# Attention and a gated feed-forward block on one core: K stacked SBUF to SBUF in eight transfers a batch, new orders of work, and the last pair's GELU output split by two engines

## The reference

```python
x = x + tanh(g_xattn) * xattn(layernorm(x), ctx)      # softmax(q k^T / 4) v, then wo, biases
x = x + tanh(g_ffn) * ffn(layernorm(x))
# ffn: gelu(x w1 + b1) w2 + b2, times the sum of the two best router weights (renormalised)
```

## Time and profile before

| | us |
|---|---|
| median of three runs | 735.21 |
| the profiled execution, its own time | 734.14 |
| its span | 732.1 |
| TensorE busy in the span | 696.4 (95%) |
| VectorE busy | 514.4 (70%) |
| ScalarE busy | 402.5 (55%) |
| GpSimd busy | 321.3 (44%) |

### The profile page before, as it was taken

One profiled execution on the slowest core, in us unless ns is written; L12 is line 12 of the kernel. 1 busy time (PEld: TensorE's weight loads), 2 busy tenths in 40 slices (PEclk: granted clock), 3 DMA queues, 4 the chain that ended last, 5 costly groups with the idle time before them and its releaser, 6 DMA issues.

```text
span 732.1 us, 20618 instructions
## 1 busy us (share of the span) xinstructions
PE 696.4 (95%) x7648; PEld 652.3 (89%) x7648; DVE 514.4 (70%) x1298; ACT 402.5 (55%) x800; POOL 321.3 (44%) x476
## 2 busy tenths in 40 slices
PE   3688999999999999999999999999999999999987
PEld 2566888999999999999999999999999999988966
DVE  6378788777776777776777777777677777766422
ACT  2124666465564646556564746556474655656753
POOL 4313436444434545434344544343454543424246
PEclk9979999999999999999999999999999999999999
DMA  4868789866748585764658486684758576450000
GB/s 146 179 198 169 187 189 224 155 170 137 178 104 174 125 187 132 171 167 124 158 111 206 103 187 154 129 190 110 165 122 182 139 171 150 104 93 3 15 1 27
DMA packets 84021, 103.21 MB, mean 141 GB/s; under 512 B 9589, under 2 KB 79570, under 8 KB 83922
## 3 DMA queue, kind: packets, MB, share of 16 engines
q1 hardware_dynamic: 83282, 101.12, 59.9%
q10 hardware_dynamic: 640, 0.77, 0.5%
HBM read 65.05 MB, written 34.05 MB: 135 GB/s over the span
## 4 chain that ended last, share of the span: by engine, by line
PE 87%; DVE 4%; ACT 2%; issue 2%; POOL 2%; SPq 1%; DMA 1%; ACTq 0%; POOLq 0%; DVEq 0%
PE P L921 42%; PE S L951 13%; PE T L963 11%; PE OT L978 11%; PE P L1004 4%; PE TR L987 2%; PE TR L1060 1%; DVE NEGM L764 1%; PE TR L1043 1%; ACT PROBS L678 1%; PE TR L994 1%; PE TR L936 1%; DVE XN L832 1%; PE TR L1028 1%; DMA QS<-q_parts 1%
## 5 line engine op out<-in xcount | busy, mean ns | idle before, releaser
L764 DVE TENSOR_REDUCE NEGM<-S 112x1 f32<-112x375 f32 x512 | 267.3, 539 | 73.4 <-PE S L951 71.3
L678 ACT ACTIVATE PROBS<-T 125x448 f32<-125x448 f32 x384 | 196.2, 543 | 106.0 <-PE T L963 98.4
L951 PE MATMUL S<-KS,QS 96*112 96x376 f32 x512 | 181.7, 361 | 9.6 <-DVE NEGM L764 6.3
L963 PE MATMUL T<-QS,KS 98*125 98x224 f32 x768 | 150.6, 282 | 3.1 <-ACT PROBS L678 1.7
L963 PEld LDWEIGHTS T<-QS,KS 98*125 98x125 f32 x768 | 129.3, 188 | 10.0 <-ACT PROBS L678 4.6
L582 POOL CAST HT_HI<-HG 128x224 fp32r<-128x224 f32 x128 | 47.3, 369 | 152.0 <-ACT HG L701 144.0
L951 PEld LDWEIGHTS S<-KS,QS 96*112 96x112 f32 x512 | 91.3, 180 | 23.5 <-DVE NEGM L764 13.0
L566 POOL CAST CT_HI<-CTRAW 128x750 fp32r<-128x750 f32 x31 | 25.1, 810 | 161.7 <-DMA CTRAW<-in_ctxT 151.0
L584 POOL TENSOR_TENSOR HT_LO<-HG,HT_HI 128x224 fp32r<-128x224 f32 x128 | 85.2, 666 | 10.3
L978 PE MATMUL OT<-PROBS,VA 125*17 125x112 f32 x3072 | 87.6, 260 | 0.0
L701 ACT ACTIVATE HG<-P,B 128x224 f32<-128x224 f32 x128 | 57.2, 447 | 53.4 <-PE P L921 52.2
(11 more groups left out here) (113 smaller groups left out, 1496.8 us busy)
## 6 DMA issues: line engine op xcount, KB each, us to landing
KS<-k_parts SPq DMA_DIRECT2D x90, 375.0 KB, 7.1
CTRAW<-in_ctxT SPq DMA_DIRECT2D x32, 375.0 KB, 3.5
k_parts<-KHI SPq DMA_DIRECT2D x30, 375.0 KB, 3.9
k_parts<-KLO SPq DMA_DIRECT2D x30, 375.0 KB, 4.5
QS<-q_parts SPq DMA_DIRECT2D x96, 112.0 KB, 4.9
X<-in_x SPq DMA_DIRECT2D x16, 224.0 KB, 3.6
q_parts<-QHI SPq DMA_DIRECT2D x32, 112.0 KB, 2.4
q_parts<-QLO SPq DMA_DIRECT2D x32, 112.0 KB, 2.3
```

What stands on the lines that cost most here:

```text
L678: act.activation(PT[0:KN, k, pp * 4 * SQ:(pp + 1) * 4 * SQ], T_BANK[i % 2][0:KN, 0:4 * SQ], ACT.Exp, scale=SCALE).then_inc(exp_done, 1)
L764: dve.tensor_reduce(NEGM[:, b.par, i:i + 1], S_BANK[i % 2][0:SQ, 0:SK], AX.X, ALU.max, negate=True).then_inc(max_done, 1)
L951: pe.matmul(S_BANK[i % 2][0:SQ, 0:SKP], QS[0:96, i, b.ring * SQ:(b.ring + 1) * SQ], KS[0:96, b.ring, i // 2, :], start=True, stop=True).th ...
L963: mm = pe.matmul(T_BANK[i % 2][0:KN, r * 2 * SQ:(r + 1) * 2 * SQ], KS[0:98, prv.ring, pair, k * KN:(k + 1) * KN], QS[0:98, 2 * pair:2 * pa ...
```

## The change

**K.** KHI and KLO get 376 columns as KS has. Every batch's K is moved directly from SBUF to SBUF, by four transfers for the high part, each of 32 source partitions written twice to 64 destination partitions, and four for the low part. The stages `ks` and `kl` and the DRAM scratch are gone, `kd` issues the moves on SP (`ka` on ScalarE for batch 0). For that, the rows are laid out anew: low in rows 0 to 31, each high row twice in rows 32 to 95, QS to fit, and the heads' order in V, NEGM and WO follows (`head`).

**Q.** QS is laid out by pair of batches and by half; its loads are as many as before (six a pair) with rows of 448 numbers in place of 224.

**Start.** The first loads are stages (`ld`) in the table, in another order. The clearing is cut into pieces that are stages too (`zp`, `zq`, `zr`, `zi`, `zh`, `zy`, `zv`, `zo`), and each user waits for its piece. w1 and w2 come in eight parts of 512 columns through HG (`lw`, `w`), whose low parts are made by GpSimd, as is that of wv.

**Orders.** Both tables are new throughout.

**The last pair.** For batches 30 and 31 GpSimd splits the even eighths of the GELU output and VectorE the odd ones.

```diff
 def move_k(engine, b, high):
+    for p in (0, 2, 1, 3):
+        slots = KS[32 if high else 0:96 if high else 32, b.ring, DC * p:DC * (p + 1), :]
+        part = (KHI if high else KLO)[32 * p:32 * p + 32, :, :].rearrange("p c n -> p (c n)").bitcast(F32)
+        if high:
+            part = part.unsqueeze(1).to_broadcast([32, 2, DC * SKP])
+        engine.dma_start(slots.rearrange("p c n -> p (c n)").bitcast(F32),
+                         part).then_inc(khi_moved if high else klo_moved, 16)
...
-                    if op == "ks" and nn.exists:
...
-                    if op == "kl" and nn.exists:
...
+                    if op == "kd" and nn.exists:
+                        held(sp, sp_passed, (st_ready, nn.count(12, -36)),
+                             (khi_done if i == 0 else klo_done, nn.count(2, 2)))
+                        move_k(sp, nn, i == 0)
...
+                    if op == "lw":
+                        src, raw_in, _, _ = w_part(i)
                         if i:
-                            sp.wait_ge(w2_split, 2 * i)
+                            sp.wait_ge(w_split, 2 * i)
+                        load(raw_in, src, w_loaded)
...
+                    if op == "w":
+                        _, raw_in, high, low = w_part(i)
+                        pool.wait_ge(w_split, 2 * i + 1)
+                        pool.tensor_tensor(low, raw_in, high.bitcast(F32), ALU.subtract).then_inc(w_split, 1)
...
-                    if op == "lo" and pg.exists:
+                    if op == "lo" and pg.exists and not (pg.k == LAST_PAIR and i % 2):
...
+                    if op == "lo" and pg.k == LAST_PAIR and i % 2:
+                        n = i // 2 + 1
+                        if i == 1:
+                            dve.wait_ge(dn_ready, pg.group(GB))
+                        dve.wait_ge(gelu_done, pg.group(FC, i + 1))
+                        dve.tensor_copy(HT[0][:, i, :], HG[:, i % HR, :]).then_inc(odd_high, 1)
+                        dve.wait_ge(odd_high, n)
+                        dve.tensor_tensor(HT[1][:, i, :], HG[:, i % HR, :], HT[0][:, i, :].bitcast(F32),
+                                          ALU.subtract).then_inc(odd_split, 1)
...
-    (34, """x2t dn.1+2 up.0 up.1 up.2 up.3 up.4 up.5 up.6 lo.0 lo.1 rt rx rw.0 up.7 rw.1 rw.2 dh.0 rw.3 lo.2 rw.4
-       lo.3 lo.4 rw.5 lo.5 dh.1 lo.6 lo.7 rw.6 rw.7 dn.0 dn.1"""),
+    (34, """x2t dn.0+2 lo.6+2 rt dn.1+2 lo.7+2 rx rw.0 up.0 up.1 lo.0 rw.1 lo.1 lo.2 up.2 up.3 lo.3 rw.2 rw.3
+       rw.4 up.4 up.5 lo.4 lo.5 up.6 lo.6 ol-1 rw.5 rw.6 up.7 lo.7 dh.0 rw.7 dh.1 dn.0 dn.1"""),
```

More of the change, by code:

```diff
@@ L46 @@
 LAG = 4
+LAST_PAIR = NB - GB
 RING = 4
@@ L395, in move_k @@
-        def move_k(engine, b, row):
-            part, moved = (KLO, klo_moved) if row == 1 else (KHI, khi_moved)
-            for p in range(4):
-                engine.dma_start(KS[32 * row:32 * row + 32, b.ring, p:NPAIR:4, 0:SK].bitcast(F32),
-                                 part[32 * p:32 * p + 32, :, :].bitcast(F32)).then_inc(moved[b.k], 16)
+        THIRD = NH * SQ
+        WK_IN, WV_IN, WQ_IN = raw(0, DC, D), raw(THIRD, DC, D), raw(2 * THIRD, DC, D)
+        W_IN = HG[:, :, :].rearrange("p r n -> p (r n)")[:, 0:W_PART]
@@ new lines, in w_part, with head @@
+        def w_part(i):
+            if i < 4:
+                c, n = i % 2, slice(W_PART * (i // 2), W_PART * (i // 2 + 1))
+                return w1[c * 128:(c + 1) * 128, n], W_IN, W1[0][:, c, n], W1[1][:, c, n]
+            c = slice(2 * (i - 4), 2 * (i - 3))
+            return (w2[c.start * 128:c.stop * 128].rearrange("(c p) n -> p c n", p=128),
+                    W_IN.rearrange("p (c n) -> p c n", c=2), W2[0][:, c, :], W2[1][:, c, :])
+        def head(h):
+            return 2 * NPAIR // DC * (h // 2 % DC) + 2 * (h // 2 // DC) + h % 2
@@ new lines, in move_k @@
+        def move_k(engine, b, high):
+            for p in (0, 2, 1, 3):
[5 more added lines that the diff above has]
+                                 part).then_inc(khi_moved if high else klo_moved, 16)
@@ L672, in step @@
                         if prv.k == 0 and i == 0:
-                            for split in (wk_split, wq_split, wv_split, w1_split):
+                            for split in (wk_split, wq_split, wv_split):
                                 act.wait_ge(split, 2)
@@ L730, in step @@
                     bank = P_BANK[BANKS.get((now.k, stage), 0)]
-                    if op in SPLIT:
+                    if op == "zp":
+                        for part in CT:
+                            dve.memset(part[:, :, :, SK:SKP].bitcast(F32), 0.0).then_inc(pads_zeroed, 1)
+                    if op == "zq":
+                        dve.memset(QS[:, 0, 1, :, :].bitcast(F32), 0.0).then_inc(qs_high_zeroed, 1)
+                    if op == "zo":
+                        dve.memset(OT[:, :], 0.0).then_inc(ot_zeroed, 1)
+                    if op in SPLIT and op in LOW_ON_DVE:
                         raw_in, parts, _, split = SPLIT[op]
```

355 lines of the change are left out of this document (176 added, 179 removed).

## The result

The changed kernel takes 712.92 us (median of four runs, 711.34 to 717.17), against 734.88 of the kernel before beside it: a ratio of 0.970, with a 95% interval of 0.965 to 0.975. The forecast was 716. Its profiled execution took 713.49 us, with a span of 711.6. Six runs more on another chip gave 712.36 (ratio 0.970, 0.967 to 0.973).

A forecast was written before the change was run, and what follows sets the result against it. TensorE was taken to bound the middle, with gains only at the start and end. Terms -4.8 + 0.7 - 8.3 + 0 - 9 + 3 - 0.7 = -19.1 us gave a 713.0 us span, forecast 716, range 705 to 733.

The forecast's parts named there:

- The start: Up to the first score product: -4.8 us, to 29.5 from 34.3, with wk and context loaded first and less clearing.
- six Q loads by 24.9, and 4.53 us later it is 29.5: Last step of the start: Q loads issued by 24.9 us, landing 4.53 us later, set the first score product.
- Batch 0's scores: First score product to batch 0's `mt`: +0.7 us, 13.5 for 12.8, with 65 matmuls in place of 34.
- 16 maxima, five V biases and some 2.5 us more: 13.2 us: VectorE's work during batch 0's scores: maxima by 0.54 us, V biases by 0.42; taken as 13.5 us.
- The ramp: Batch 0's to batch 5's `mt`: -8.3 us, 96 for 104.3, as the splits of w1 and w2 leave VectorE.
- 29 for these two: In the ramp, batches 1 and 2 together take 29 us, at VectorE's pace of some 14 us each.
- The middle: Batch 5's to batch 29's `mt`: K's new way gives 0, bounds -6 to +6; TensorE waits for no K there.
- The last pair's scores: Batch 29's to 31's `mt`: -9 us, 27 at 0.087 a matmul; then to the last `x2t`: +3, 26.5 for 23.5.
- The end: Last pair's `x2t` to the end: -0.7 us, 19.2 for 19.9, with GELU splits shared by GpSimd and VectorE.
- The weight pieces: Rival, 0.09: SP's seven waits for w1 and w2 pieces delay K or Q by 4 us each: 744 us.
- The steady stretch: Rival, 0.08: the middle holds waits too short to see; 40.8 us a pair, 12 us more gained: 704 us.
- Only the two ends: Rival, 0.17: VectorE's 0.54 us a maximum holds close scores, so -8.3 and -6 shrink to -2 each: about 726 us.

The follow-up runs named there:

- GpSimd waits once: Changed kernel, but GpSimd starts the context split of iteration -1 only when VectorE has scaled the third pair's XN: 711.9 us, ratio 0.967.
- RSTD first: Changed kernel, but in iteration -2 GpSimd makes the second pair's variance and RSTD before the context cast, CT_LO and BO: 712.5 us, ratio 0.969.
- changed kernel again: The changed kernel once more, unaltered, in six runs: 712.4 us, ratio 0.970.
- sixteen moves: Changed kernel with each of the eight K moves of a batch cut into two of half the size: 730.3 us, ratio 0.993.
- twelve moves: The kernel before with its orders, layout and start, only K moved directly by twelve moves a batch: 817.3 us, ratio 1.109.
- XN later: Changed kernel, but VectorE scales the third pair's XN in iteration 0 between the maxima of heads 8 and 9, after KLO: 714.9 us, ratio 0.972.
- three moves: Changed kernel with XN later, GpSimd's RSTD before the context split, and ScalarE's tanh of the gates behind both K halves: 711.4 us, ratio 0.969.

## Why the prediction was right, point by point

- **The start, 29.5 for 29.1: right in size, wrong in the last wait.** The step "six Q loads by 24.9, and 4.53 us later it is 29.5" failed. TensorE's chain of waits (start us, us, what) leads through the second pair's XN and not through the Q loads:

```profile
9.87 4.65 DMA CTRAW<-in_ctxT
...
15.57 1.64 POOL CT_LO L591
17.20 0.93 POOL BO L581
...
18.65 0.73 POOL RSTD L543
19.41 0.75 DVE XN L847 x2
...
20.29 0.98 PE TR L1055 x4
21.27 4.48 PE P L943 x18
```

  I had counted GpSimd's list nowhere in this stretch. The chain goes back to the second context, which SP issues at 9.87 us behind all the first loads and which GpSimd splits before it makes RSTD. The Q loads were issued by 25.3 and landed in 2.7 to 3.3 us where I had put 4.53, so the Q path was some 1 us off being last: with XN earlier by 1.3 us the score products wait for it. That the time agreed within 0.4 us is luck. The first matmul came at 6.8 (forecast 7.5).
- **Batch 0's scores, +0.7 for +4.5: wrong.** The step was the sum "16 maxima, five V biases and some 2.5 us more: 13.2 us" of VectorE's work, with each instruction at its price alone. Without the collision it is right: 13.5, 12.9 and 13.5 us in three profiles (GpSimd waits once, RSTD first, changed kernel again). The prediction used the rule of the shared ports at the last pair and did not look for it here, though the earlier trace rows had wv's low part at 1.84 us.
- **The ramp, -8.3 for -12.3: right in sign, short by a third.** VectorE's relief, on which the term stood, brings 3.9 us. The rest is the order: 92.0 for 117.8 with the same code. The step that failed is "29 for these two": batches 1 and 2 took 24.8 us and not VectorE's pace of 14 each, while the other three took 22.3, 19.2 and 25.7 for 22, 18.5 and 26.5. TensorE is busy for 90.7 of the 92.0 us.
- **The middle, 0 for -3.2: right within its bounds.** Nothing waits for K, a pair takes 41.55 for 41.8, and the difference is the order's, since with the old one it is 41.74. The ten profiles with this order, the one with sixteen moves among them, have 498.0 to 499.7 us here, so up to 1.7 of the 3.2 us differ from one execution to another. The slack in SP's queue is at least the 4.8 us that sixteen moves used up, and it belongs to the order: in the old one twelve moves cost 5.8 us a pair.
- **The last pair's scores, -9 for -6.5; then +3 for +1.9.** Both within bounds. The 29.5 us have 28.8 of TensorE busy, so 313 matmuls cost 0.092 each there and not the 0.087 of the steady stretch, which was the wrong mean for that mix. Together they are -4.6 for -6.
- **The end, -0.7 for +0.3.** The two engines do exclude each other; the splits in turn are worth 1.5 us, and the final additions on GpSimd behind WT set the result at 708.0, which I had put on TensorE's last down projections.
- **The rivals.** The weight pieces do hold SP, but 4.4 us in two waits, where it takes seven of 2.7 to decide; in the old order SP waits 24.1 us for them, and their share of the loss was not measured apart. The steady stretch gains 3.2 us and not 12. "Only the two ends" fell with the ramp.

The sum came out 1.4 us from the span by luck, because +3.8 and -4.0 cancelled. K's way, the headline of the change, gains nothing by itself: in the old orders its eight moves leave the middle as it was, while the whole new code is 10 us slower there, since the ramp loses 13.5 us; twelve moves cost 82 us.

## What to carry to other kernels

A transfer that moves fewer bytes can still cost more queue: count the issues that stand in front of the next transfer someone waits for, and the buffer that is only free when the last has landed. Where VectorE and GpSimd work at the same time ahead of TensorE, look at the duration of each instruction in that place and not at the mean of its group; if one comes out several times longer and ends with the other engine's, let GpSimd wait for it, and look in the profile whether that wait ever acts. In this kernel it took 1.9 us off one pair of instructions (2.60 to 0.74), and the median went from 712.5 to 710.2, within the spread of the runs. Moving VectorE's instruction only moved the collision.

## What the runs showed of the hardware

- Two TENSOR_SCALAR of 112 x 256 on VectorE take 0.73 to 0.75 us alone, 2.59 beside GpSimd's CAST and CT_LO, 2.78 beside a MEMSET of KS, and 5.75 over CAST, CT_LO and a MEMSET of QS. GpSimd's CAST had started 0.08 us before the first of them in the case of 2.59 and 0.06 us behind it in that of 5.75. In both the first was held until the CAST ended (0.88 and 1.01 us for 0.41) and the second took the rest (1.80 and 4.82).
- A direct move of K takes 0.6 us of SP's queue whether it writes 47 or 188 KB (medians 0.591 and 0.605 us). Cut in half, it lands in 2.2 us for 2.7 (medians).
- TensorE's granted clock over the stretch behind the first score product was 0.69 with a wait of 5.9 us in it, 0.80 with one of 2.8, 0.89 with ones of 2.2 and 2.4 (XN later, three moves), and 1.00 where the longest was 1.1 or less.
